# Flamingo block with a two-expert layer: the order of the last sequences' steps where attention hands over to the expert tiles

## The reference

```python
x = x + tanh(g_xattn[0]) * xattn(layernorm(x), ctx, ctx)      # 16 heads of 16
x = x + tanh(g_ffn[0]) * moe(layernorm(x))

def moe(xt):
    logits = xt @ Wr + br                                      # 8 experts
    top_vals, top_idx = top_k(logits, 2)
    gate = softmax(where(picked, logits, -inf))
    h = relu(einsum('td,edh->teh', xt, W1) + b1)
    y = einsum('teh,ehd->ted', h, W2) + b2
    return einsum('ted,te->td', y, gate)
```

## Time and profile before

| | us |
|---|---|
| median of 3 runs | 817.29 (815.95 to 819.60) |
| the profiled execution | 816.96 |
| its span, first to last instruction | 814.9 |
| PE busy | 722.2 |
| DVE busy | 603.6 |
| POOL busy | 462.8 |
| ACT busy | 404.4 |

### The profile page before, as it was taken

How to read it: one execution, slowest core, us unless ns; L and a number is a source line. 1 busy time by engine, 2 the same in 40 slices (tenths; PEclk the granted TensorE clock), 3 DMA queues, 4 the chain that set the end, 5 groups by cost and what they waited for, 6 DMA issues and landing times.

```text
span 814.9 us, 21021 instructions
## 1 busy us (share of the span) xinstructions
PE 722.2 (89%) x6536; PEld 484.2 (59%) x6537; DVE 603.6 (74%) x1256; ACT 404.4 (50%) x783; POOL 462.8 (57%) x453
## 2 busy tenths in 40 slices
PE   3688989888887888877799999999999999999993
PEld 2344555554554545533477777777777777777771
DVE  5767888888888998987467777667666666776663
ACT  3266777676776767657433333333333333343430
POOL 6224544666567665446666777665556665555533
PEclk9699999999999999988899999999999999999997
DMA  6436646766666755553134323343233223232322
GB/s 191 133 114 189 189 144 193 182 179 182 160 168 183 193 162 160 145 172 118 42 104 51 49 47 45 55 55 46 47 51 51 46 46 53 42 51 42 53 34 26
DMA packets 96797, 85.43 MB, mean 105 GB/s; under 512 B 22256, under 2 KB 86000, under 8 KB 96592
## 3 DMA queue, kind: packets, MB, share of 16 engines
q1 hardware_dynamic: 80752, 65.73, 29.0%
q0 software_dynamic: 15680, 18.69, 14.7%
q10 hardware_dynamic: 288, 0.00, 0.0%
HBM read 53.61 MB, written 30.62 MB: 103 GB/s over the span
## 4 chain that ended last, share of the span: by engine, by line
PE 64%; DVE 20%; issue 9%; ACT 4%; DMA 1%; POOL 1%; another core or an unknown queue 1%; DVEq 0%; POOLq 0%; SPq 0%; ACTq 0%
PE banks L1774 22%; PE banks L1759 7%; PE banks L1761 7%; PE banks L1760 7%; DVE negmax L1124 6%; PE banks L1675 4%; PE banks L1585 3%; PE banks L1663 2%; ACT probs L933 2%; PE banks L1745 2%; PE banks L1718 2%; PE banks L1571 2%; DVE stats L1048 2%; PE banks L1702 2%; PE banks L1635 1%
## 5 line engine op out<-in xcount | busy, mean ns | idle before, releaser
L996 ACT ACTIVATE hid<-banks,b_col 128x256 f32<-128x256 f32 (+1 forms) x312 | 122.8, 453 | 212.9 <-PE banks L1761 97.7
L1774 PE MATMUL banks<-wall,hh 128*128 x568 | 205.6, 382 | 2.6 <-DVE hl L1466 2.6
L785 POOL DMA_INDIRECT out_dram<-yb,dest_idx x71 | 125.4, 1767 | 123.2 <-DVE yb L1519 111.3
L1124 DVE TENSOR_REDUCE negmax<-banks 128x4 f32<-128x1024 f32 x128 | 155.5, 1217 | 19.9 <-PE banks L1635 19.2
L933 ACT ACTIVATE probs<-banks 128x1024 f32<-128x1024 f32 x128 | 131.0, 1024 | 68.4 <-PE banks L1663 64.8
L1759 PE MATMUL banks<-xh,wall 128*128 128x256 f16 (+1 forms) x624 | 161.3, 263 | 4.0 <-DVE xl L1455 1.3
L1760 PE MATMUL banks<-xl,wall 128*128 128x256 f16 (+1 forms) x624 | 161.2, 263 | 0.0
L1761 PE MATMUL banks<-xh,wall 128*128 128x256 f16 (+1 forms) x624 | 161.2, 263 | 0.0
L1774 PE MATMUL banks<-wall,hl 128*128 x568 | 144.9, 274 | 0.0
L1675 PE MATMUL banks<-probs,vaug 128*32 128x256 f32 x1024 | 83.9, 399 | 24.6 <-ACT probs L933 15.7
L707 POOL DMA_INDIRECT token_lists<-entry,place_i x64 | 69.8, 1091 | 60.7 <-ACT probs L933 41.0
(11 more groups left out here) (201 smaller groups left out, 1164.9 us busy)
## 6 DMA issues: line engine op xcount, KB each, us to landing
raw<-in_L_ffn_W SPq DMA_DIRECT2D x16, 512.0 KB, 5.9
wst<-in_L_ffn_W SPq DMA_DIRECT2D x16, 512.0 KB, 6.4
k_parts<-kparts SPq DMA_DIRECT2D x48, 128.0 KB
q_parts<-qparts SPq DMA_DIRECT2D x48, 128.0 KB
ks<-k_parts SPq DMA_DIRECT2D x64, 96.0 KB, 2.3
qs<-q_parts SPq DMA_DIRECT2D x64, 96.0 KB, 2.2
xin<-in_x SPq DMA_DIRECT2D x16, 256.0 KB, 2.9
cin<-in_ctx SPq DMA_DIRECT2D x16, 256.0 KB, 3.2
```

What stands on the lines that cost most here:

```text
L785: nc.gpsimd.indirect_dma_start(out_rows, bass.IndirectOffsetOnAxis(dest_idx[par][:, s:s + 1], 0), yb[par][:, s, :], None, compute_op=ALU.a ...
L996: ins = nc.scalar.activation(hid[half][:, c % (HC // 2), 0:subs(j) * P], banks[:, b, c % 2 * TS:c % 2 * TS + subs(j) * P], ACT.Relu, bias= ...
L1124: nc.vector.tensor_reduce(negmax[:, c, 8 * (g // 2):8 * (g // 2) + 8].rearrange("p (m g p2) -> p m g p2", m=2, g=2)[:, :, g % 2, :], banks ...
L1774: ins = nc.tensor.matmul(dst, h_[:, c, s * P:(s + 1) * P], w_, start=(c == 0 and k == 0), stop=(c == HC - 1 and k == 1))
```

## The change

In the last body DVE does `attended_low(14)` at step 2 and not 3, and the low parts 6 and 7 of the late weights both at step 3, not at steps 2 and 4. After the bodies, PE turns sequence 15's sums ahead of 14's normalized rows, and ACT makes both copies ahead of `relu(0, e, 1)`. The turn and router of sequence 15 leave the end of step 0 and go into step 1 on PE: the turn before chunk 1, now into bank 7, the router before chunk 3, and a wait for its sum before chunk 4. On ACT the copy goes to the head of step 1. On DVE the router's sum goes behind `entries` and `carry_on`.

```diff
--- before.py
+++ after.py
@@ -865,10 +865,10 @@
                 wait(act, o_done, n)
                 nc.scalar.activation(cT[:, 0].rearrange("p m t -> p (m t)"), bank(5), ACT.Copy).then_inc(cT_evac, 1)
 
-            def norm2_T(n):
+            def norm2_T(n, at=6):
                 act.wait_ge(x2T_done, n + 1)
                 wait(act, lg_done, n)
-                nc.scalar.activation(x2T[:].rearrange("p m t -> p (m t)"), bank(6), ACT.Copy).then_inc(x2T_evac, 1)
+                nc.scalar.activation(x2T[:].rearrange("p m t -> p (m t)"), bank(at), ACT.Copy).then_inc(x2T_evac, 1)
 
             def late_high(i):
                 e, w, half = LATE[i]
@@ -1000,6 +1000,8 @@
             def step(j, t, i):
                 if there(j, 1):
                     e = act.value_load(tile_expert[0:1, ds(entry_of(j + 1) if isinstance(j, int) else j + 1, 1)], min_val=0, max_val=E - 1)
+                    if isinstance(j, int) and j == 1:
+                        norm2_T(NB - 1, 7)
                     for b in range(2):
                         relu(j + 1, e, b)
                 if there(j, 2):
@@ -1007,9 +1009,7 @@
                 if there(j, 1):
                     for b in range(2, 4):
                         relu(j + 1, e, b)
-                if isinstance(j, int) and j == 0:
-                    norm2_T(NB - 1)
-                elif isinstance(j, int) and j == 2:
+                if isinstance(j, int) and j == 2:
                     spread(NB // 2 - 1)
                 elif isinstance(j, int) and j == TABLES_AT:
                     act.wait_ge(table_ready, 6)
@@ -1017,9 +1017,9 @@
             act.wait_ge(table_ready, 2)
             e = act.value_load(tile_expert[0:1, 0:1], min_val=0, max_val=E - 1)
             relu(0, e, 0)
+            attended_T(NB - 1)
+            norm2_T(NB - 2)
             relu(0, e, 1)
-            norm2_T(NB - 2)
-            attended_T(NB - 1)
             relu(0, e, 2)
             high_x(1, 1)
             relu(0, e, 3)
@@ -1355,14 +1355,14 @@
             def body(t, par):
                 m = 2 * t + par
                 maxima, ahead, turns, attention, post, weights, splits, judged = parts_of(m)
-                late_at_step = {NB - 1: {1: 0, 2: 1, 4: 2, 5: 3, 7: 4}, NB: {1: 5, 2: 6, 4: 7}}.get(m, {}) if isinstance(m, int) else {}
+                late_at_step = {NB - 1: {1: (0,), 2: (1,), 4: (2,), 5: (3,), 7: (4,)}, NB: {1: (5,), 3: (6, 7)}}.get(m, {}) if isinstance(m, int) else {}
                 listing, gating, q = lists_at(m, par, LEAD), lists_at(m, par, LEAD + 1), t - 2
                 for w in range(8):
                     if gating and w == 0:
                         places(q)
                     if w == 1 and ahead:
                         k_low(m + 1)
-                    if w == 3 and post:
+                    if w == (2 if isinstance(m, int) and m == NB else 3) and post:
                         attended_low(m - 2)
                     if maxima:
                         reduce(m, w)
@@ -1430,8 +1430,8 @@
                             low(1, t, par)
                     if w == 5 and isinstance(m, int) and m == 0:
                         output_weights()
-                    if w in late_at_step:
-                        late_low(late_at_step[w])
+                    for x_ in late_at_step.get(w, ()):
+                        late_low(x_)
                     if isinstance(m, int) and m == NB - 1 and w == 3:
                         early_table()
 
@@ -1546,9 +1546,9 @@
                 if there(j, -1) and after_small:
                     result(j - 1, t + (i - 1) // 2, 1 - i, 0, e)
                 if fixed and j == 0:
-                    router(NB - 1, 1, 7)
                     entries(NB // 2 - 2)
                     carry_on(NB // 2 - 2)
+                    router(NB - 1, 1, 7)
                     listed_top(NB // 2 - 1)
                 elif fixed and j == TABLES_AT:
                     dve.wait_ge(table_ready, 6)
@@ -1705,9 +1705,9 @@
                 if c == C - 1:
                     ins.then_inc(o_done, 1)
 
-            def norm2_T(n):
+            def norm2_T(n, at=6):
                 pe.wait_ge(xn2_ready, 2 * (n + 1))
-                turn(xn2b, 6, x2T_done)
+                turn(xn2b, at, x2T_done)
 
             def router(n, rank_of=None, at=5):
                 pe.wait_ge(x2T_evac, n + 1)
@@ -1861,8 +1861,8 @@
             turn_out(n, 1)
             first(0, 0, e, 2)
             first(0, 0, e, 3)
+            attended_T(n)
             norm2_T(n - 1)
-            attended_T(n)
             first(0, 0, e, 4)
             first(0, 0, e, 5)
             router(n - 1, None, 7)
@@ -1879,12 +1879,18 @@
                 if there(j, -1):
                     e2 = pe.value_load(tile_expert[0:1, ds(entry_of(j - 1) if isinstance(j, int) else j - 1, 1)], min_val=0, max_val=E - 1)
                 if isinstance(j, int) and j == 1:
-                    pe.wait_ge(x2T_evac, NB)
-                    pe.wait_ge(lg_evac, NB)
+                    pe.wait_ge(x1_ready, 2 * NB)
                 if isinstance(j, int) and j in (0, 2):
                     pe.wait_ge(xl_ready, j + 2)
                     ranks(NB // 2 - 2 + j // 2)
                 for c in range(HC):
+                    if isinstance(j, int) and j == 1 and c == 1:
+                        pe.wait_ge(lg_evac, NB - 1)
+                        norm2_T(NB - 1, 7)
+                    elif isinstance(j, int) and j == 1 and c == 3:
+                        router(NB - 1, None, 7)
+                    elif isinstance(j, int) and j == 1 and c == HC // 2:
+                        pe.wait_ge(lg_evac, NB)
                     if there(j, 1):
                         first(j + 1, 1 - i, e1, c)
                     if there(j, -1):
@@ -1896,10 +1902,7 @@
                         if isinstance(j, int) and j in (1, 3):
                             pe.wait_ge(rank_evac, NB // 2 - 1 + j // 2)
                         gathered_T(j + 2, t + 1, i)
-                if isinstance(j, int) and j == 0:
-                    norm2_T(NB - 1)
-                    router(NB - 1, None, 7)
-                elif isinstance(j, int) and j == TABLES_AT:
+                if isinstance(j, int) and j == TABLES_AT:
                     pe.wait_ge(table_ready, 6)
                 elif isinstance(j, int) and j == TILE_LEAD - 1:
                     pe.wait_ge(xl_ready, TILE_LEAD + 2)
```

## The result

The change makes the kernel faster by 0.68%. In 17 runs each on one chip its median is 812.42 us (810.07 to 816.02) beside 817.79 us (815.95 to 821.5) for the kernel before: a ratio of 0.9932, 95% interval 0.992 to 0.9944, or 5.6 us. The forecast was 811.7 us, a gain of 5.5.

What follows compares the result with a forecast made beforehand. PE, busy 89% of the span, was taken to bound the kernel, with its idle time in the seam before the tiles to be gained. Terms 2.9 + 0.8 + 1.8 = 5.5 us gave 811.7 us, range 806.8 to 816.4.

Steps and rivals of the forecast that it cites:

- B: Last turns after the bodies: sums turned first, both copies ahead of the relu; 0.8 us gain, nearer the late-signal end.
- C: Last router moved into tile 2's first layer: work stays, idle goes; 1.8 us gain, bounds -0.1 to 2.0.
- A: DVE's order in the last body: tile 0's first layer starts 2.9 us sooner, bounds 2.0 to 3.9.
- 2.0 us: Last body: cT's low part starts near 386.15, not 388.11, after late_low(5) ends at 385.9.
- second term: Before tile 0: late_low(7) moved out of the way of tile 0's low_x on DVE, worth 0.9 us.
- upper end: Last turns, prompt signals: output product starts at T+6.9, not T+9.1, and at full clock; gain 3.6 us.
- lower end: Last turns, signals late as before: x2T's copy and the router follow cT's copy; loss of 1.5 us in all.
- R3: Tile 2: PE's wait for the last logits at chunk 4 makes the kernel slower, 821.8 us at 11 us lateness; chance 0.06.
- R1: Seam: prompt signals and full clock, 9.3 us gained, 807.9 us; chance 0.18.
- R2: Seam hangs on POOL: late signals or gathered rows hold PE; 1.4 to 3.2 us gained, about 814.7; chance 0.30.
- R4: Tiles: the freed time is given back there, as DVE starts tile 0's result later; about 817 us; chance 0.06.
- clock rule: Seam: idle gaps bring half rate back, so both half-clock stretches should go, sum near 8; transposes may lower the clock instead.

Runs made afterwards that it cites:

- c_only: The kernel before with only the change's hunks of the last router (turn and router inside tile 2's first layer): 807.82 us, ratio 0.9949.
- all_again: The whole change once more, against the kernel before on a second chip: 807.14 us, ratio 0.9931.
- res_early: The kernel after with POOL's addition of the output bias for sequence 14 moved from body 16 to 15: 808.03 us, ratio to before 0.9941.
- b_only: The kernel before with only the new order of the last turns and copies: 813.41 us, ratio 1.0009.
- no_b: The changed kernel with the order of last turns and copies undone: 806.82 us, ratio to the kernel before 0.9925.
- a_only: The kernel before with only the change's hunks in DVE's bodies: 809.90 us, ratio 0.9957.
- fill kernels: The kernel before with 14 useless PE products in the waits around the last router, run on two chips: ratios 0.9981 and 0.9979.
- low_only: The kernel before with only attended_low(14) a step sooner, late_low(6) and (7) left in place: 810.43 us, ratio 0.9975.
- res_g3: res_early with POOL's gather of tile 3's rows moved ahead of the last normalization: 811.32 us, ratio to the kernel before 0.9908.

## Why the prediction was right, point by point

**The sum** was right, 5.5 for 5.6 us, and tile stage and tail kept their length, so the seam's gain reached the end. That it was right to 0.1 us is in part luck: B was put too high, C too low by more than half, A perhaps (2.9 lies inside its interval), and the parts measured alone add to 6.9 us (known to 2.4), not to 5.5. The parts ran alone only on chips where ACT's signals came prompt. The whole gained as much where they came late (0.9932) as where they came prompt (0.9931), so the lateness that the prediction weighed between its two ends did not decide the gain.

**A, forecast 2.9, measured 3.5 (2.3 to 4.8).** Right in size, and in that the two moved passes fit ahead of x1b. The step "**2.0 us**" from `late_low(5)`'s end at 385.9 was wrong: it took that pass at 1.22 us and left out POOL's addition beside it. In c_only against all_again the low part moved by 4.5 - 3.0 = 1.5 us, one pass; res_early is the case that was forecast. Tile 0's first product came forward by 1.9 us there (12.9 to 11.0), and not by 2.9: beside the 0.5 us of the low part, the second term, 0.9 us, was 0.4, since it let tile 0 start 0.1 us behind PE's last attention product where 0.5 pass. What makes 3.5 of 1.9 us is not known; the interval reaches down to 2.3.

**B, forecast a gain of 0.8 between -1.5 and 3.6, measured -0.7 (-2.2 to 0.7).** The step that failed is the choice between the two ends, and the upper end. The upper end held the old order to its late profile (T+9.1) where with prompt signals the old order is as fast as the new, T+6.5: PE's own products fill the stretch. The lower end came true as an order (x2T behind cT, the output product 0.5 later in the kernel after); what it costs is not known, since b_only and no_b ran where the signals were prompt. The lags of the five late profiles show no difference of the orders: 9.1 and 9.9 in the old, 9.6, 8.9 and 9.1 in the new. And the reason for the lateness fell: POOL's train of four sends starts 1.0 to 1.8 us behind tile 0's first product in every profile of this case, with the copy 0 to 0.4 us behind its turn in eight profiles and 2.4 to 3.1 in five. The five are all the ones from the two sets of runs in which the kernel before takes 818 to 819 us, the eight those from the sets of 813. So lateness goes with the chip, in the thirteen profiles here. What it is stays open: matmul ends are modelled, so products that really ended later look the same as late signals.

**C, forecast 1.8 between -0.1 and 2.0, measured 4.1 (2.7 to 5.5).** Mis-sized. The mechanism was right: no wait on logits in tile 2, so R3 did not happen, and the waits named went. The term counted 1.8 us of idle time in one profile; without late signals the old order idles 2.4 us (a_only) and C's lag falls by 2.6 (21.0 to 18.4). What is left of 4.1 is about 1.5 us. The fill kernels, in which PE is busy in the pauses around the router (lag 20.5 in both), gain about as much, 1.6 us, which points at the clock as what the term left out. That link is argued, from two intervals that reach 1.0.

**The rivals.** R1's premise, prompt signals, held on two of the chips, and gave B nothing. R2's premise, late signals beside POOL's train, held in the profile after, and its price did not: the runs of that chip gained 5.6 us, not 1.4 to 3.2. Its gathered rows do hold PE up, but only once the seam is shorter still (no_b, res_early), and when issued soon behind transfers of SP's. R4 was not seen: from the last `ranks` to the end all profiles take 381.5 to 383.2 us.

**The clock rule** of "TensorE: Matmul & The Clock Gate" in the Trainium skill, that gaps bring half rate back, agrees with the 0.50 at 406 to 412 us of the kernel after, behind the 2.1 us wait; whether pauses as short as those around the last router, 0.4 to 1.3 us, fall under it the rows leave open, with 0.57 behind them in b_only and 1.00 in before, a_only and low_only. By that half, the prediction said, both half-clock stretches of the seam should go; in the profile after they did not, and the wait for x2T had stayed. Its second half, on transposes, no run here shows.

## What to carry to other kernels

A wait read from one profile is worth what stands behind it with everything else prompt: before pricing a reordering, lay the engine's own work end to end and see whether any order of it would wait. Before calling a moved operation ready "when the one ahead ends", look what GpSimd runs at that moment. And when a stage gets shorter, look at every transfer that another queue issues in it and that does not move along: here a load of 1 MB, with two of 256 KB behind it, came to stand just ahead of 128 gathered rows.

## What the runs showed of the hardware

- The same kernel took 812.67, 813.15, 817.79 and 818.89 us in four sets of runs on at least three chips, and in the slower pair ACT's first copy at the seam starts 2.4 to 3.1 us behind the modelled end of the PE work that it needs, in the faster pair 0 to 0.4.
- A DVE pass of 1.22 us took 3.12 when GpSimd's addition of 1.29 us started 0.7 us after it; a onehot of about 0.2 us took 1.04 in the same place.
- In res_early, gathered rows were issued 6.5 us before the turn that waited for them; the DMA engines were busy for 0.96 to 1.01 of the first 3.3 us of these. With the gather 3.1 us ahead of that load (res_g3) that turn did not wait.
- Fourteen products added in pauses did not make the kernel slower (0.9981 and 0.9979).
